# A graph-network kernel: the second stage's split messages get their own buffer count, and their makers run two pieces ahead

## The reference, cut to what matters

```python
h = layernorm(x)
# graph layer: out[dst] += w * support[src], plus the node itself
support = h @ W1
out = segment_sum(w * support[src], dst) + support
out = relu(batchnorm(out))             # statistics over all 12,500 nodes
out = segment_sum(w * (out @ W2)[src], dst) + out @ W2
x = x + out
# then x = x + MoE(layernorm(x)), 8 experts, top 2
```

## Time and profile before

| | us |
|---|---|
| three runs | 4903.26, 4911.59, 4928.97 |
| median | 4911.59 |
| the profiled execution, its own time | 4917.16 |
| its span in the trace | 4915.4 |

### The profile page before, as it was taken

The page is one execution under the profiler, slowest core; times in us unless marked ns, Lnnn a source line. Parts: engine busy times, 40 slices in busy tenths (PEclk is TensorE's granted clock), DMA queues, the critical chain, the costliest instruction groups (busy, mean ns, idle before and its releaser), DMA issues.

```text
span 4915.4 us, 85592 instructions
## 1 busy us (share of the span) xinstructions
PE 3975.2 (81%) x27967; PEld 3425.1 (70%) x27967; DVE 3685.4 (75%) x7827; ACT 2979.6 (61%) x6003; POOL 3320.7 (68%) x3177
## 2 busy tenths in 40 slices
PE   0588888888868888887578888888888888888898
PEld 0477777777756666665247777777777777777778
DVE  6699898999958777877446776777677667776776
ACT  3488888888844443445236665666666666666655
POOL 0367776677657666763667777777777777777761
PEclk6699999999989999999559999999999999999999
DMA  7788888887788888886423334333433343334331
GB/s 199 237 299 291 298 295 299 302 299 274 259 280 287 286 284 277 291 290 217 139 88 111 109 111 122 113 109 112 124 111 112 110 123 112 109 113 122 109 96 40
DMA packets 346462, 928.66 MB, mean 189 GB/s; under 512 B 51066, under 2 KB 158066, under 8 KB 346018
## 3 DMA queue, kind: packets, MB, share of 16 engines
q0 software_dynamic: 153216, 483.15, 29.3%
q1 hardware_dynamic: 192170, 439.40, 28.5%
q10 hardware_dynamic: 632, 0.55, 0.0%
HBM read 597.06 MB, written 325.83 MB: 188 GB/s over the span
## 4 chain that ended last, share of the span: by engine, by line
PE 33%; DMA 15%; ACT 14%; issue 13%; POOL 13%; DVE 11%; SPq 1%; DVEq 0%; ACTq 0%; POOLq 0%
DMA X<-h,tabT 11%; POOL X L1196 9%; ACT A L806 6%; PE ps L1352 5%; PE ps L1141 4%; PE ps L744 3%; PE ps L1373 3%; PE ps L745 2%; POOL mL L1096 2%; PE ps L702 2%; PE ps L701 2%; PE ps L728 2%; DVE gL L1213 2%; PE ps L955 2%; PE ps L1235 2%
## 5 line engine op out<-in xcount | busy, mean ns | idle before, releaser
L1196 POOL DMA_INDIRECT X<-h,tabT x1800 | 1884.5, 1047 | 659.9 <-issue 417.7
L1224 ACT ACTIVATE gH<-X,tabT 128x256 fp32r<-128x256 f32 x1200 | 589.6, 504 | 661.8 <-DMA X<-h,tabT 532.9
L855 POOL DMA_INDIRECT msgd<-A,tabT x464 | 610.3, 1315 | 367.0 <-ACT A L806 293.0
L806 ACT ACTIVATE A<-ps,A 128x256 f32<-128x256 f32 x1856 | 745.5, 498 | 181.0 <-PE ps L745 180.8
L1213 DVE SCALAR_TENSOR_TENSOR gL<-X,tabT,gH 128x256 fp32r<-128x256 f32 x1200 | 560.4, 479 | 373.1 <-ACT gH L1224 355.4
L744 PE MATMUL ps<-winH,DT 128*128 128x256 f32 x1856 | 517.1, 310 | 104.0 <-issue 82.7
L1237 PE MATMUL ps<-gH,s 128*125 128x256 f32 x1200 | 396.0, 331 | 212.7 <-ACT gH L1224 112.3
L1079 ACT ACTIVATE mH<-L 128x1280 fp32r<-128x1280 f32 (+1 forms) x267 | 307.6, 1164 | 384.7 <-PE ps L1141 219.7
L745 PE MATMUL ps<-winL,DT 128*128 128x256 f32 x1856 | 477.3, 289 | 0.0
L1096 POOL TENSOR_TENSOR mL<-L,mH 128x256 fp32r<-128x256 f32 x267 | 365.0, 1367 | 163.8 <-ACT mH L1079 104.2
L1220 ACT ACTIVATE X<-X,tabT 128x256 f32<-128x256 f32 x600 | 302.0, 503 | 281.1 <-DMA X<-h,tabT 279.8
(11 more groups left out here) (255 smaller groups left out, 10500.6 us busy)
## 6 DMA issues: line engine op xcount, KB each, us to landing
L<-msgd SPq DMA_DIRECT2D x200, 650.0 KB, 5.7
L<-msgd SPq DMA_DIRECT2D x200, 520.0 KB, 5.4
A<-sbd SPq DMA_DIRECT2D x58, 805.0 KB, 6.2
msgd<-A SPq DMA_DIRECT2D x100, 390.0 KB
X<-h,tabT POOLq DMA_INDIRECT x1800, 2.8
winR<-h SPq DMA_DIRECT2D x116, 128.0 KB
A<-in_x SPq DMA_DIRECT2D x10, 1120.0 KB
h<-A SPq DMA_DIRECT2D x10, 1120.0 KB
```

The lines of the kernel that those rows point to most:

```text
L806: e.activation(M[:, n, 0:F], psum[4 + v % 4][:, (n % 2) * F:(n % 2 + 1) * F], ACT.Identity, scale=M[:, n, F + 2:F + 3]).then_inc(evc, 1)
L855: e.indirect_dma_start(msgd, bass.IndirectOffsetOnAxis(ap=idxI[g % 4][:, t:t + 1], axis=0), msg[g % 3][:, t * 4 * RW:(t + 1) * 4 * RW], No ...
L1196: e.indirect_dma_start(B.G[c % GR], None, h2, bass.IndirectOffsetOnAxis(ap=tab3[:, c, 0:1].bitcast(I32), axis=0)).then_inc(gat[c % GR], 16)
L1224: e.activation(B.gH[c % HR2][:, :], B.G[c % GR], ACT.Identity, scale=w_).then_inc(g_hi, 1)
```

## The change

- `SRD = 4`: S gets four buffers, chosen by `u % 4`; making S for piece u waits for piece u-4.
- The buffers of mH and mL stay three, but are counted over split pieces only (`terms_slot`). Making a term waits for the split piece three split pieces back (`terms_free`), which is piece u-4 or u-5.
- ACT and DVE run with a lead of two: they make piece u+2 before they look at what follows piece u.
- The first `acc_load` stands behind the first two pieces' loads; the later ones stand where SP reaches block 5, 15, ..., 85, not 0, 10, ..., 80.
- `aT` has one buffer during this stage. The batch-norm step that follows it uses `L[0]` as its second one, and waits for all table copies first.

```diff
-LR, HR = 6, 3
+LR, HR, SRD = 6, 3, 4
+def terms_slot(u):
+    return (split_upto(u, whole) - 1) % HR
+def terms_free(e, u, r_mm):
+    v = [x for x in range(u) if not whole(x)][-HR:]
+    if len(v) == HR:
+        e.wait_ge(r_mm, v[0] + 1)
...
         def act_dense1_y(e, i, aT):
-            if i >= 2:
-                e.wait_ge(d1_mm, 2 * (i - 1))
+            if i:
+                e.wait_ge(d1_mm, 2 * i)
...
-                self.S = [st(f"S{i}", PC * R, FR) for i in range(HR)]
-                self.aT = [st(f"aT{i}", 1024) for i in range(2)]
+                self.S = [st(f"S{i}", PC * R, FR) for i in range(SRD)]
+                self.aT = [st("aT0", 1024), self.L[0][:, 0:1024]]
...
         def sp_read(e, B):
-            acc_load(e, 0)
             for u, (b, k, n) in enumerate(PIECES):
-                if k == 0 and b % XB == 0 and b + XB < NB:
+                if k == PC + PC - 1 and b == 0:
+                    acc_load(e, 0)
+                if k == 0 and b % XB == XB // 2 and b + XB < NB:
                     acc_load(e, b // XB + 1)
...
         # act_read
-                if u >= HR:
-                    e.wait_ge(r_mm, u - HR + 1)
+                terms_free(e, u, r_mm)
                 e.activation(H, L3[:, :, 0:F], ACT.Copy).then_inc(r_hi, 1)
             high(0)
+            high(1)
             for u, (b, k, n) in enumerate(PIECES):
-                if u + 1 < NU:
-                    high(u + 1)
+                if u + 2 < NU:
+                    high(u + 2)
...
         # dve_read
-                if u >= HR:
-                    e.wait_ge(r_mm, u - HR + 1)
+                if u >= SRD:
+                    e.wait_ge(r_mm, u - SRD + 1)
                 e.tensor_tensor(S3, ...).then_inc(r_sel, 1)
                 if not whole(u):
                     e.wait_ge(r_hi, split_upto(u, whole))
+                    terms_free(e, u, r_mm)
                     e.tensor_tensor(Lo[:, 1:n, :], ...).then_inc(r_lo, 1)
             parts(0)
+            parts(1)
             for u, (b, k, n) in enumerate(PIECES):
-                if u + 1 < NU:
-                    parts(u + 1)
+                if u + 2 < NU:
+                    parts(u + 2)
...
                 act_read(e, RB)
+                e.wait_ge(r_tab, NU)
                 act_bn(e, RB.aT)
```

More of the change, by code:

```diff
@@ L954, in pe_dense1_y @@
                 for k in range(2):
-                    m = e.matmul(psum[q][:, 0:n * R], W1s[:, k, m_ * P:(m_ + 1) * P], aT[i % 2][:, k * 512:k * 512 + n * R],
+                    m = e.matmul(psum[q][:, 0:n * R], W1s[:, k, m_ * P:(m_ + 1) * P], aT[:, k * 512:k * 512 + n * R],
                                  start=k == 0, stop=k == 1)
@@ L960, in act_dense1_y @@
             b0, n = SBS[i]
-            if i >= 2:
-                e.wait_ge(d1_mm, 2 * (i - 1))
+            if i:
+                e.wait_ge(d1_mm, 2 * i)
             for k in range(2):
                 e.wait_ge(d1_tr, 2 * i + k + 1)
-                e.activation(aT[i % 2][:, k * 512:k * 512 + n * R], psum[2 + (4 * i + k) % 6][:, 0:n * R], ACT.Copy).then_inc(d1_cp, 1)
+                e.activation(aT[:, k * 512:k * 512 + n * R], psum[2 + (4 * i + k) % 6][:, 0:n * R], ACT.Copy).then_inc(d1_cp, 1)
             for m_ in range(2):
@@ L1049, in of @@
                 L3 = self.L[u % LR].rearrange("p (k r) -> p k r", r=RW)[:, 0:n, :]
-                H, Lo = (t[u % HR][:, 0:n * F].rearrange("p (k f) -> p k f", f=F) for t in (self.mH, self.mL))
-                return n, L3, H, Lo, self.S[u % HR][:, 0:n * R].rearrange("p (k f) -> p k f", f=R)
+                H, Lo = (t[terms_slot(u)][:, 0:n * F].rearrange("p (k f) -> p k f", f=F) for t in (self.mH, self.mL))
+                return n, L3, H, Lo, self.S[u % SRD][:, 0:n * R].rearrange("p (k f) -> p k f", f=R)
         def acc_load(e, i):
@@ L1076, in high @@
                 e.wait_ge(ldm[u % LR], 16 * (u // LR + 1))
-                if u >= HR:
-                    e.wait_ge(r_mm, u - HR + 1)
+                terms_free(e, u, r_mm)
                 e.activation(H, L3[:, :, 0:F], ACT.Copy).then_inc(r_hi, 1)
             high(0)
+            high(1)
             for u, (b, k, n) in enumerate(PIECES):
-                if u + 1 < NU:
-                    high(u + 1)
+                if u + 2 < NU:
+                    high(u + 2)
                 if k == PC and b and b in STARTS:
-                    act_dense1_y(e, STARTS[b] - 1, B.aT)
-            act_dense1_y(e, NS - 1, B.aT)
+                    act_dense1_y(e, STARTS[b] - 1, B.aT[0])
+            act_dense1_y(e, NS - 1, B.aT[0])
         def pool_read(e, B):
@@ L1145, in pe_read @@
                     e.wait_ge(r_add, b)
-                    pe_dense1_y(e, STARTS[b] - 1, B.aT)
+                    pe_dense1_y(e, STARTS[b] - 1, B.aT[0])
             e.wait_ge(r_add, NB)
-            pe_dense1_y(e, NS - 1, B.aT)
+            pe_dense1_y(e, NS - 1, B.aT[0])
         class Last:
@@ L2022, in general @@
                 for i in range(NS):
-                    act_dense1_y(e, i, g_aT)
+                    act_dense1_y(e, i, g_aT[0])
                 act_bn(e, g_aT)
@@ L2089, in general @@
                 for i in range(NS):
-                    pe_dense1_y(e, i, g_aT)
+                    pe_dense1_y(e, i, g_aT[0])
                 pe_bn(e, g_aT)
```

2 lines of the change are left out of this document (removed).

## The result

Four executions of the changed kernel gave a median of 4866.26 us (4859.28 to 4870.74), four of the kernel before 4913.06 us; the recorded ratio is 0.9884, with a 95% interval of 0.9864 to 0.9905. It isn't the quotient of the two medians, which is 0.9905 and lies at the edge of the interval; on 4913 us the interval means a gain of 47 to 67 us. The medians stand 47 us apart, where I forecast 57 (4854) and a range of 4800 to 4898. The profiled execution took 4861.84 us by its own time, with a span of 4860.0.

What follows compares the result with a forecast made beforehand. DVE was taken to set the pace between dense steps and stand idle at them; 40 + 8.5 + 10 + 6 - 8 = 57 us off 4917.2 gives 4860, 4854 as run median, range 4800 to 4898 (own range 4835 to 4882).

Steps and rivals of the forecast that it cites:

- The dense step: At 25 dense steps, DVE work moves into its wait before the statistics: 40 us plus 8.5; idle 132 to 80 to 95.
- the moved piece: DVE makes piece u+2 before waiting for the statistics at a dense step: 25 x 1.61 = 40 us won.
- the moved sum: The block's sum falls between piece e+2 and the dense step, while PE still multiplies: 25 x 0.34 = 8.5 us won.
- The block ends: DVE's 17.1 us wait for PE at block ends shrinks with one more piece made first: 10 us won, bounds 0 and 17.
- The start: The first two pieces land before the row loads at the stage's start: 6 us won, bounds 3 and 8.
- The row loads and messages inside the stage: Four uncovered row loads, asked for sooner, cost 6 us and one extra load 2: 8 us lost, bounds 0 and 25.
- The hindrance by POOL: DVE and POOL subtractions exclude each other; DVE's one-hot and subtraction means were to hold within 3%.
- POOL takes it back: Rival: filled DVE gaps make DVE pay 40 us more hindrance, gain 17, time 4895; chance 0.19 shared with a stall that only moves.
- The sum: All terms of the change together: 40 + 8.5 + 10 + 6 - 8 = 57 us gained.
- The period: Time between dense steps falls from 33.5 to about 31.3 us; 31 to 32 was a sign of being right.
- The rival "ring": Six message buffers become the bound, as whole pieces return theirs only after PE: 100 us lost, time 4955; chance 0.07.
- frees more: Rival: DVE's gaps shrink to PE's bound of 28.8 us per period, gain 118, time about 4795; chance 0.14.

Runs made afterwards that it cites:

- the run with the shortest stage: Changed kernel with POOL's subtraction column given to DVE, run again on another chip: ratio 0.9826 to the kernel before, stage 817.3 us.

## Why the prediction was right

*The dense step.* I wrote 40 us for the moved piece and 8.5 for the moved sum; the idle time before the statistics fell by 132.1 - 89.4 = 42.7. The mechanism was right, the size a little large; 89.4 is inside the 80 to 95 that I had forecast. Over the 26 steps that is 1.64 us each, where I had 1.61 for the piece and 0.34 for the sum. The runs don't part the two.

*The block ends.* Taken 10, bounds 0 and 17; measured 16.2 (17.1 to 0.9). With one more piece made first, PE is late at one block end and not at 63.

*The start.* Taken 6, measured 7.2 in DVE's waits (16.84 to 9.6). The first one-hot starts at 1385.98 (I said 1387), the third at 1394.86 (I said 1393 to 1395).

*The row loads and messages inside the stage.* Charged 8 us. DVE's wait for messages without the start rose from 20.1 to 26.0 us, so 6. The runs split it otherwise than I did: with lead of two and the old places it is 30.9, so there the lead costs 11, and the new places give 5 back. I had charged a cost for the places too. Where the waits stand I had right: the uncovered loads at blocks 15, 35, 55 and 75 cost 4.72, 6.11, 2.96 and 4.46 us.

*The hindrance by POOL.* Here the sum was wrong: I took the mean duration of a DVE piece as unchanged ("the mean price moves along") and gave 3% as the limit for right. The subtraction held (1.257 to 1.247 us), the one-hot did not (0.879 to 0.916, 4%). 15 us more on one-hots, 3 less on subtractions. In the time that DVE is busy that makes 8 us (710.5 to 718.4). That is part of the rival "POOL takes it back", to which I had given 40 us; it took 8. With a lead of one, the buffers and row loads changed, the one-hots are at 0.882, so their growth came with the lead. The run without POOL's column shows the price in full: one-hots at 0.735 us on the mean. My undisturbed value for them was 0.73.

*The sum.* 42.7 + 16.2 + 7.2 - 5.9 - 2.7 (mH, 5.9 to 8.6) - 7.9 (busy) = 49.6, with 50.3 measured on the stage and 47 on the time. DVE's idle time alone fell by 58 us, near my whole sum of 57, but that my terms met it is in part luck: the dense step gave 6 less than I put, the block ends 6 more, start and messages 3 more, mH 3 less. What I left out are the 8 us that DVE works longer. By the runs, the lead is worth 37 us where my terms for it come to 52 (40 + 8.5 + 10, less 6 for messages), and the places of the row loads 12 where I had 4 (6 for the start less 2). Two errors of opposite sign brought the total near.

*The period.* I said 31.3 us after 33.5, and 31 to 32 as a sign of being right. The mean went from 35.4 to 33.6, 1.8 less, and the median from 34.8 to 32.9, where my terms give 2.0 + 0.4. Only 3 of the 23 periods lie between 31 and 32. The starting value was one pair of steps, which was a short one; the difference was nearly met, the level was not, and this sign failed. So did that of the one-hot's mean.

*The rival "ring".* It did not come with a lead of two: messages cost DVE 6 us more, not 100. With a third piece ahead on ACT 50 us were lost, in part to messages behind row loads, and filling DVE's gap in the dense step won 10 us of 89 at best. The reason that I gave against it, that DVE's lead melts away between dense steps, fits the 26 us but was not tested by itself.

*The rival "frees more".* I had thought PE's 28.8 us per period to be the floor for it. No run came near; in the run with the shortest stage, 817 us, most periods lie between 30.3 and 32.3 us.

What stays open: which part of the last 140 us of DVE's waits is the latency of loads in a ring of six, and which the order of ACT and PE in the dense step. The runs show only that the sum did not fall when either was reordered (147 us against 143, and with ACT three ahead 195).

## What to carry to other kernels

Where an engine's idle time stands at one place in its program order, count what it could do there: one more piece of work before the wait is worth about its own duration (1.64 us less idle time per step for pieces of 1.61 on the mean), and here it needed no new buffer. The second step of the same kind has to be checked against the supply: ACT one piece further ahead lost 50 us, because it then stood before a load with PE waiting behind it. And a column handed from a busy engine to an idle one is a gain only if they can run together: taking POOL's share back made DVE's total shorter, 648 us for 693, with more work in it.

## What the runs showed of the hardware

DVE's one-hot and POOL's subtraction hinder each other as the subtractions do: without POOL's column the one-hots' mean is 0.735 us, with it 0.879 to 0.937 from run to run. The Trainium skill, page "SBUF — State Buffer", section "Who interferes with whom", names DVE instructions with two SBUF inputs and GpSimd instructions that read SBUF; both kinds here are of that sort, and the trace agrees. The table copies read SBUF too; in the run without the column it is they that are stretched, as told above.

The message loads run at 417 GB/s in a window of the changed kernel with hardly anything else (1394 to 1400 us), the busy share being 1.02; with a row load among them it is 301 GB/s at a share of 1.06:

```profile
1384.00:1394.00 10.00, 6.24 (x18) 4.67 (x18) 3.16 (x3) 1.27 (x1) 2.48 (x3) 0.51 1.06 301
1394.00:1400.00 6.00, 2.81 (x14) 2.63 (x14) 4.65 (x5) 3.31 (x3) 3.73 (x4) 0.78 1.02 417
```

A stall of PE can cost more than its length. In the run with ACT three ahead PE was idle for 9.2 us at the first dense step, and its eight products then took 5.70 us, not 3.63, at a granted clock of 0.50 (1.2 GHz), where it had been 1.00 (2.4 GHz) before the pause:

```profile
1420.00:1429.00 9.00, 8.15 (x51) 7.15 (x49) 9.00 (x12) 4.16 (x4) 7.74 (x10) 1.00 0.98 320
...
1439.00:1443.00 4.00, 3.91 (x5) 1.85 (x6) 1.46 (x2) 0.21 (x2) 1.52 (x2) 0.50 0.54 222
```
